# A selective-scan, top-1 expert and feed-forward layer: a new written order of the steps in the steady batches and in the last two and a half

## The reference

```python
delta = softplus(x @ Wd + bd); Bm = x @ WB + bB; Cm = x @ WC + bC; A = -exp(A_log)
# for each token t, state h of 128 x 16:
bar_A = exp(minimum(d_t * A, 2.0)); bar_B = clip(d_t * B_t, -2, 2)
h = clip(bar_A * h + bar_B * x_t, -100, 100)
y = sum(h * C_t, over the 16 states) + x_t * D_param
# for each token y: the most likely of 4 experts
routing = softmax(y @ Wr + br); e = argmax(routing)
moe = (silu(y @ up_w[e] + up_b[e]) @ down_w[e] + down_b[e]) * routing[e]
out = layernorm(y + moe) * ln_w + ln_b
x = layernorm(x + out)
x = layernorm(x + (silu(x @ wg) * (x @ wu)) @ wdn)    # weights are integers / 127
```

## Time and profile before

| | us |
|---|---|
| median of 3 timed runs | 859.77 |
| the three runs | 859.2, 859.77, 875.19 |
| the profiled execution, whole | 854.52 |
| its span, first to last instruction | 852.7 |
| busy: PE, DVE, ACT, POOL | 652.5, 706.2, 517.1, 558.3 |
| first scan to last scan's end | 34.5 to 718.0 |

### The profile page before, as it was taken

One profiled execution on the slowest core, in us unless ns is written; L12 is line 12 of the kernel. 1 busy time (PEld: TensorE's weight loads), 2 busy tenths in 40 slices (PEclk: granted clock), 3 DMA queues, 4 the chain that ended last, 5 costly groups with the idle time before them and its releaser, 6 DMA issues.

```text
span 852.7 us, 14265 instructions
## 1 busy us (share of the span) xinstructions
PE 652.5 (77%) x4267; PEld 529.3 (62%) x4322; DVE 706.2 (83%) x1458; ACT 517.1 (61%) x970; POOL 558.3 (65%) x452
## 2 busy tenths in 40 slices
PE   3366567876789768995889778986988668889686
PEld 1144345864588547874688557964787447778555
DVE  3699999889999999799999999999979999324452
ACT  5274084777577946775777847784678413575534
POOL 1257458658875887578865886588766886525442
PEclk9587696997799959996799869995999859799988
DMA  3333346785467637674578536764667465375410
GB/s 110 123 127 121 127 146 208 244 265 163 146 221 241 204 118 229 201 214 169 171 236 249 177 120 223 237 210 154 209 190 228 140 198 185 107 219 181 132 37 26
DMA packets 82088, 149.32 MB, mean 175 GB/s; under 512 B 9404, under 2 KB 51144, under 8 KB 81992
## 3 DMA queue, kind: packets, MB, share of 16 engines
q1 hardware_dynamic: 69192, 135.13, 49.7%
q0 software_dynamic: 4096, 8.40, 3.1%
q10 hardware_dynamic: 8704, 4.72, 1.9%
HBM read 132.80 MB, written 15.40 MB: 174 GB/s over the span
## 4 chain that ended last, share of the span: by engine, by line
PE 32%; DVE 30%; issue 13%; POOL 12%; ACT 6%; DMA 5%; DVEq 1%; SPq 1%; another core or an unknown queue 0%; POOLq 0%; ACTq 0%
DVE state L1304 8%; DVE state L1318 7%; PE psU L767 6%; POOL prod L1350 5%; PE psT L781 5%; PE psY L637 4%; DVE psB L1299 4%; PE psD L661 3%; POOL rows_in L1371 3%; DMA xT_sb<-in_xT 2%; DMA weights<-in_w_pack 2%; DVE attn L1271 2%; PE psU L808 2%; PE psB L631 2%; PE psU L810 2%
## 5 line engine op out<-in xcount | busy, mean ns | idle before, releaser
L1350 POOL TENSOR_TENSOR prod<-state,c_wide 128x1024 f32<-128x1024 f32 x128 | 302.0, 2367 | 129.7 <-DVE state L1318 109.1
L1299 DVE TENSOR_TENSOR psB<-dx,psB 128x512 f32<-128x512 f32 x256 | 166.7, 684 | 19.3 <-PE psB L631 9.6
L631 PE MATMUL psB<-parts,sel 128*128 128x512 bf16 x202 | 94.0, 470 | 109.7 <-DVE state L1318 65.0
L893 ACT ACTIVATE decay<-delta,a_sb 128x1024 f32<-128x1024 f32 x128 | 141.4, 1141 | 50.1 <-DVE state L1318 48.8
L637 PE MATMUL psY<-ident,prod 128*128 128x128 f32 x1024 | 169.5, 323 | 2.6 <-DVE state L1318 1.5
L1318 DVE TENSOR_TENSOR_SCAN state<-decay,state,psB 128x512 f32<-128x512 f32 x128 | 163.3, 1276 | 8.7
L637 PEld LDWEIGHTS psY<-ident,prod 128*128 128x128 f32 x1024 | 152.0, 170 | 11.6 <-issue 7.9
L1304 DVE TENSOR_TENSOR_SCAN state<-decay,psB 128x512 f32<-128x512 f32 x128 | 155.2, 1213 | 0.1
L934 ACT ACTIVATE hid<-psU,weights 128x128 f32<-128x128 f32 x352 | 100.2, 370 | 50.1 <-PE psU L767 48.4
L631 PEld LDWEIGHTS psB<-parts,sel 128*128 128x128 bf16 x256 | 26.3, 103 | 160.7 <-DVE state L1318 92.7
L767 PE MATMUL psU<-yT_sorted,weights 128*128 128x128 f32 x704 | 95.8, 280 | 10.1 <-DMA weights<-in_w_pack 4.1
(11 more groups left out here) (163 smaller groups left out, 1030.0 us busy)
## 6 DMA issues: line engine op xcount, KB each, us to landing
c_wide<-c_rows SPq DMA_DIRECT2D x128, 512.0 KB, 5.0
weights<-in_w_pack SPq DMA_DIRECT2D x88, 514.0 KB, 4.0
xT_sb<-in_xT SPq DMA_DIRECT2D x8, 512.0 KB, 4.6
y_sorted<-rows_in SPq DMA_DIRECT2D x16, 256.0 KB, 3.3
xt<-in_x SPq DMA_DIRECT2D x8, 512.0 KB, 5.6
...
```

What stands on the lines that cost most here:

```text
L631: pe.matmul(tokens(psB, c, h), sel[:, s, :], parts[:, c.n % 2, h * HALF:h * HALF + c.hw], start=True, stop=True).then_inc(b_ready, 1)
L893: nc.scalar.activation(decay[:, g % NDECAY, w], delta[:, n % 2, w], ACT.Exp, scale=a_sb[:, s:s + 1]).then_inc(decay_ready, 1)
L1299: v.tensor_tensor(tokens(psB, c, h), dx[:, n % 2, h * HALF:h * HALF + c.hw], tokens(psB, c, h), ALU.mult).then_inc(inp_ready, 1)
L1350: g_.tensor_tensor(prod[:, g % NPROD, w], state[:, g % NSTATE, w], c_wide[:, g % NC, w], ALU.mult).then_inc(prod_ready, 1)
```

## The change

Only the ten lists change; no step is added or removed, and each step's instructions and waits stay as they are. Against the list before, a steady batch n (scans of n, expert part of n-1, feed-forward of n-2, preparation of n+1) differs so:

- DVE: b_max goes from behind scan(9) to behind scan(8); centre(1) from ahead of scan_rest(9) to behind scan_rest(10), ahead of bc_low; router_pick, stats(0,2) and aggr(0,2) go ahead of scan_rest(11); dx from behind scan(13) to behind scan_rest(12).
- POOL: prod(2) two gathers earlier; gather(7) ahead of prod(5); x_shift(0) behind prod(12), x_shift(1) behind prod(13).
- ACT: z_copy and softplus later among the decays; decay(11) ahead of norm(0,1), decay(12) behind it, widen ahead of x_low(0); decay(14) from behind silu(3) to ahead of sort_copy(0); x_scaled from behind result(0) to behind sort_copy(2); sort_copy(1) and bc_mid ahead of silu(2); x_high(1) ahead of silu(5).
- SP: c(8) ahead of rows; weights(0) to weights(2) together behind c(4); x later; c rows a place earlier or later.
- PE: b_turn ahead of spread(5,0); ff_up(0,5) ahead of sort_turn(0); sort_turn(1), sort_turn(2), spread(10,1), spread(11,0) one or two places earlier; down(4) ahead of add(10); spread(14,0) from ahead of ff_up(1,1) to behind ff_up(1,4), past b_spread(1) and ff_down(1).

In the last lists (batches 5, 6, 7): combine(0), stats and aggr of batch 5 go from behind scan(14) and scan_rest(15) into scans 10 to 12 of batch 7, combine(1) behind the last scan_rest; SP issues store(0) of batch 6 behind weights(10) and store(1) behind weights(0) of batch 7; PE does ff_down(0) of batch 6 behind ff_up(0,1), ff_down of batch 7 behind ff_up(h,3). The other moves there are of a place or two.

The diff, cut to its core ("..." marks what is left out):

```diff
 PE_ORDER = [
...
-    (-2, "spread", 14, 0), (-4, "ff_up", 1, 1), (-3, "down", 6), (-3, "up", 7), (-1, "b_spread", 1),
...
+    (-2, "spread", 9, 1), (-4, "ff_up", 0, 5), (-3, "sort_turn", 0), (-3, "up", 0), (-2, "spread", 10, 0),
...
+    (-4, "ff_up", 1, 0), (-4, "ff_up", 1, 1), (-3, "down", 6), (-3, "up", 7), (-1, "b_spread", 1),
+    (-4, "ff_up", 1, 2), (-4, "ff_down", 1), (-4, "ff_up", 1, 3), (-4, "ff_up", 1, 4), (-2, "spread", 14, 0),
...
 ACT_ORDER = [
-    (-5, "sort_copy", 2), (-5, "silu", 3), (-4, "decay", 14), (-4, "decay", 15), (-6, "norm", 1, 1),
...
-    (-3, "decay", 12), (-5, "x_low", 0), (-2, "widen"), (-3, "decay", 13), (-5, "gate", 0, 0), (-5, "gate", 0, 1),
-    (-5, "gate", 0, 2), (-4, "sort_copy", 0), (-4, "silu", 0), (-4, "silu", 1), (-4, "result", 0), (-2, "x_scaled"),
-    (-4, "silu", 2), (-2, "bc_mid"), (-4, "result", 1), (-4, "sort_copy", 1), (-4, "result", 2),
...
+    (-6, "gate", 0, 2), (-4, "decay", 14), (-5, "sort_copy", 0), (-5, "silu", 0), (-5, "silu", 1), (-5, "result", 0),
+    (-5, "sort_copy", 1), (-3, "bc_mid"), (-5, "silu", 2), (-5, "result", 1), (-5, "sort_copy", 2), (-3, "x_scaled"),
+    (-5, "result", 2), (-5, "silu", 3), (-4, "decay", 15), (-6, "norm", 1, 1), (-5, "result", 3), (-5, "silu", 4),
...
 DVE_ORDER = [
...
-    (-2, "scan", 9), (-1, "b_max"), (-4, "ff_mul", 0, 2), (-4, "centre", 1), (-2, "scan_rest", 9), (-2, "scan", 10),
-    (-2, "scan_rest", 10), (-1, "bc_low"), (-4, "affine", 1), (-4, "stats", 1, 1), (-4, "aggr", 1, 1),
...
-    (-2, "scan", 12), (-2, "scan_rest", 12), (-2, "scan", 13), (-1, "dx"), (-3, "router_pick"), (-2, "scan_rest", 13),
...
+    (-2, "scan", 8), (-1, "b_max"), (-4, "stats", 1, 0), (-2, "scan_rest", 8), (-4, "aggr", 1, 0),
...
+    (-2, "scan", 10), (-2, "scan_rest", 10), (-4, "centre", 1), (-1, "bc_low"), (-4, "affine", 1),
+    (-4, "stats", 1, 1), (-4, "aggr", 1, 1), (-2, "scan", 11), (-1, "bound", 0), (-3, "router_pick"),
+    (-4, "stats", 0, 2), (-4, "aggr", 0, 2), (-2, "scan_rest", 11), (-2, "scan", 12), (-2, "scan_rest", 12),
+    (-1, "dx"), (-2, "scan", 13), (-2, "scan_rest", 13), (-1, "bound", 1), (-1, "over"), (-4, "ff_mul", 1, 0),
...
 POOL_ORDER = [
...
-    (-6, "rstd", 1, 1), (-4, "prod", 10), (-6, "rstd", 0, 2), (-5, "x_shift", 0), (-4, "prod", 11), (-4, "prod", 12),
...
+    (-5, "prod", 9), (-4, "bound_input"), (-7, "rstd", 1, 1), (-5, "prod", 10), (-7, "rstd", 0, 2), (-5, "prod", 11),
+    (-5, "prod", 12), (-6, "x_shift", 0), (-5, "prod", 13), (-6, "x_shift", 1), (-5, "prod", 14), (-7, "rstd", 1, 2),
...
 SP_ORDER = [
...
-    (-6, "weights", 2), (-6, "rows"), (-5, "c", 8), (-5, "c", 9), (-5, "c", 10), (-6, "weights", 3), (-5, "c", 11),
...
+    (-6, "c", 6), (-6, "c", 7), (-6, "c", 8), (-7, "rows"), (-6, "c", 9), (-7, "weights", 3), (-6, "c", 10),
...
 PE_LAST = [
...
-    (-1, "down", 10), (-2, "ff_down", 0), (-2, "ff_up", 0, 0), (-2, "ff_up", 0, 1), (-2, "ff_up", 0, 2),
...
+    (-1, "down", 10), (-2, "ff_up", 0, 0), (-2, "ff_up", 0, 1), (-2, "ff_down", 0), (-2, "ff_up", 0, 2),
...
 DVE_LAST = [
...
-    (-3, "combine", 0), (-3, "combine", 1), (-1, "scan_rest", 14), (-1, "scan", 15), (-1, "scan_rest", 15),
...
+    (-1, "scan_rest", 9), (-1, "scan", 10), (-3, "combine", 0), (-1, "scan_rest", 10), (-1, "scan", 11),
+    (-3, "stats", 0, 0), (-1, "scan_rest", 11), (-1, "scan", 12), (-3, "aggr", 0, 0), (-1, "scan_rest", 12),
...
+    (-1, "scan_rest", 15), (-2, "router_pick"), (-3, "combine", 1), (-3, "stats", 1, 0), (-3, "centre", 0),
...
 SP_LAST = [
...
-    (-2, "weights", 6), (-2, "weights", 7), (-2, "store", 0), (-2, "weights", 8), (-2, "weights", 9),
...
+    (-2, "weights", 7), (-2, "weights", 8), (-2, "weights", 9), (-2, "weights", 10), (-2, "store", 0), (-1, "rows"),
+    (-2, "x"), (-1, "weights", 0), (-2, "store", 1), (-1, "weights", 1), (-2, "store", 2), (-1, "weights", 2),
...
```

More of the change, by code:

```diff
@@ L70 @@
 PE_ORDER = [
-    (-2, "spread", 11, 0), (-3, "down", 2), (-2, "spread", 11, 1), (-3, "sort_turn", 2), (-3, "up", 3),
-    (-4, "ff_down", 0), (-4, "ff_part", 0, 0), (-1, "b_spread", 0), (-4, "ff_part", 0, 1), (-2, "add", 8),
-    (-4, "ff_part", 0, 2), (-3, "down", 3), (-2, "add", 9), (-2, "spread", 12, 0), (-3, "up", 4),
-    (-2, "spread", 12, 1), (-3, "up", 5), (-2, "add", 10), (-3, "down", 4), (-2, "spread", 13, 0), (-4, "x_turn", 1),
-    (-2, "spread", 13, 1), (-3, "up", 6), (-2, "add", 11), (-4, "x_rest", 1), (-3, "down", 5), (-4, "ff_up", 1, 0),
@@ new lines @@
+    (-2, "spread", 9, 1), (-4, "ff_up", 0, 5), (-3, "sort_turn", 0), (-3, "up", 0), (-2, "spread", 10, 0),
+    (-3, "up", 1), (-2, "spread", 10, 1), (-3, "down", 0), (-3, "sort_turn", 1), (-3, "up", 2), (-3, "down", 1),
+    (-2, "spread", 11, 0), (-3, "sort_turn", 2), (-2, "add", 7), (-3, "down", 2), (-2, "spread", 11, 1),
+    (-4, "ff_down", 0), (-3, "up", 3), (-1, "b_spread", 0), (-4, "ff_part", 0, 0), (-2, "add", 8),
+    (-4, "ff_part", 0, 1), (-4, "ff_part", 0, 2), (-3, "down", 3), (-2, "spread", 12, 0), (-3, "up", 4),
@@ L104 @@
 ]
 DVE_ORDER = [
-    (-4, "stats", 0, 0), (-2, "scan_rest", 4), (-4, "aggr", 0, 0), (-2, "scan", 5), (-4, "centre", 0),
-    (-4, "affine", 0), (-4, "stats", 0, 1), (-2, "scan_rest", 5), (-4, "aggr", 0, 1), (-2, "scan", 6),
-    (-2, "scan_rest", 6), (-2, "scan", 7), (-1, "delta"), (-2, "scan_rest", 7), (-4, "combine", 1), (-2, "scan", 8),
-    (-4, "stats", 1, 0), (-2, "scan_rest", 8), (-4, "aggr", 1, 0), (-4, "ff_mul", 0, 0), (-4, "ff_mul", 0, 1),
-    (-2, "scan", 9), (-1, "b_max"), (-4, "ff_mul", 0, 2), (-4, "centre", 1), (-2, "scan_rest", 9), (-2, "scan", 10),
@@ L116 @@
-    (-2, "scan", 15), (-2, "scan_rest", 15), (-1, "scan", 0), (-1, "scan_rest", 0), (-1, "scan", 1),
-    (-1, "scan_rest", 1), (-1, "scan", 2), (-2, "router_shift"), (-1, "scan_rest", 2), (-2, "slots"), (-1, "scan", 3),
-    (-3, "combine", 0), (-1, "scan_rest", 3), (-1, "scan", 4),
+    (-2, "scan", 4), (-4, "stats", 0, 0), (-2, "scan_rest", 4), (-4, "aggr", 0, 0), (-2, "scan", 5),
+    (-4, "centre", 0), (-4, "affine", 0), (-4, "stats", 0, 1), (-2, "scan_rest", 5), (-4, "aggr", 0, 1),
+    (-2, "scan", 6), (-2, "scan_rest", 6), (-2, "scan", 7), (-1, "delta"), (-2, "scan_rest", 7), (-4, "combine", 1),
@@ new lines @@
+    (-3, "affine", 0), (-3, "stats", 0, 1), (-3, "aggr", 0, 1), (-1, "router_shift"), (-3, "aggr", 1, 0),
+    (-1, "slots"), (-3, "centre", 1), (-3, "affine", 1), (-3, "ff_mul", 0, 0), (-3, "stats", 1, 1),
+    (-3, "aggr", 1, 1), (-3, "ff_mul", 0, 1), (-3, "ff_mul", 0, 2), (-3, "stats", 0, 2), (-3, "aggr", 0, 2),
+    (-3, "ff_mul", 1, 0), (-3, "ff_mul", 1, 1), (-3, "ff_mul", 1, 2), (-2, "combine", 0), (-2, "stats", 0, 0),
+    (-2, "aggr", 0, 0), (-2, "centre", 0), (-2, "affine", 0), (-2, "stats", 0, 1), (-2, "aggr", 0, 1),
```

202 lines of the change are left out of this document (97 added, 105 removed), and 6 rows, old and new, of the table SP_ORDER.

## The result

| | before | after |
|---|---|---|
| median of six runs, us | 861.64 (859.2 to 875.19) | 868.23 (866.6 to 871.69) |
| profiled execution, us | 854.52 | 871.69 |
| its span, us | 852.7 | 869.9 |

The ratio is 1.0092, with a 95% interval of 1.0063 to 1.0121. By the 2% bound this is no change, but the interval lies wholly above 1, and 868.2 is above the forecast's range (838 to 863). The two profiled executions stand 17.2 apart, the medians 6.6: the profiled execution of before is faster than each of its six timed ones, and that of after is the slowest of its six. So the profiles are read for places, and what a place costs is taken from timed ratios. Two of the experiments (e6 and e10) had a disturbed profiled execution; only their times are used.

The account below looks back on a forecast made before the run. DVE was taken as near its limit in the steady periods, PE not far behind, the tail a PE, ACT and weight-DMA chain. Gains of 10.0 + 1.5 = 11.5 from 854.5 gave 843.0, plus 5.3 for the median: 848, range 838 to 863.

Parts of the forecast that it names:

- the stall of 2.1: DVE's affine(1), stretched 2.1 us by GpSimd's bound_input each steady period; forecast gone, with 0.1 us margin, chance 0.40.
- The first rival: Bound_input enters between affine's third and fourth step, so the stall stays: 852.5, 858 as a median; chance 0.33.
- the group's 1.32 is no longer ahead: DVE before bc_low: scan_rest(10) ends at about 425.9, since centre(1)'s 1.32 us now comes behind it.
- the first two batches: Start of the run, ahead of the steady periods: change of 0, within 1 us.
- delta in the steady periods: DVE's delta meets the end of prod(5), now behind gather(7): a cost of 0.2 us a period.
- The 49 table loads: ACT table changes rise from 39 to 49, 1283 ns each; cost nothing if ACT's idle covers them.
- dx's wait: DVE's dx is freed of prod(12): 1.1 us won, but for nothing, since bound(1) waits for PE's b_spread(1).
- The last lists: Tail after the steady periods: -1.5 us, from -4 to +3, by weight DMAs and ff_down(0); last scans nothing.
- a period gains 2.0: Each steady period is 2.0 us shorter, bounds 0 to 3.2; five periods give 10.0.
- the third rival: Slower: bound(0) waits for bound_input after late x_scaled, through uncovered table changes and PE's lower clock; 864.5, median 870; chance 0.14.
- the second: Rival: more goes than one stall (dx's 1.1, PE's lower clock, tail); gain 23, 831.5, 837 as a median; chance 0.13.
- PE's clock behind down(3): PE's fall to 1.2 of 2.4 GHz in two of five periods may go: 0 to 4 us, taken as 0.

Follow-up runs that it names:

- e6: Kernel after with gather(7) back behind prod(5), in five batches: 864.3 us, 0.9833 of before.
- e10: Kernel after with affine(1) ahead of bc_low, x and both x_shifts in their old places, gather(7) back behind prod(5): 859.0 us, no ratio.
- e4: Kernel after with decay(14) ahead of decay(15), 39 table loads again: 868.7 us, 1.0081 of before.
- e9: Kernel after with x_scaled one place later on ACT, behind result(2): 856.7 us, 0.9922 of before.
- e3: Kernel after with the x DMA and both x_shifts in their old places: 864.7 us, 1.0014 of before.
- e14: Kernel before with centre(1) behind scan_rest(10), in five batches: 872.1 us, 1.0112 of before.
- e15: Kernel after with affine(1) ahead of bc_low and centre(1), stats(0,2), aggr(0,2), router_pick in their old places: 883.2 us, 1.0254 of before.
- e11: Repeat of e6, kernel after with gather(7) back behind prod(5): 859.4 us, 0.9967 of before.
- e2: Kernel after with affine(1) ahead of bc_low, in five batches: 856.4 us, 0.9940 of before.
- e5: Kernel before with the change's last lists, steady lists old: 863.0 us, 0.9979 of before.
- e1: Kernel before with affine(1) ahead of bc_low in the five steady batches: 849.5 us, 0.9871 of before.
- e17: Kernel after with affine(1) ahead of bc_low and the x DMA and both x_shifts in their old places: 849.9 us, 0.9854 of before.

## Why the prediction was wrong

**The step that failed** is "If it comes behind the last affine step's start (429.4), the stall of 2.1 is gone ... I take this case". From bc_low's end I had put bound_input at 0.9 and the last step's start at 1.0; they came at 0.65 and 0.83 (bc_low ends 438.78; 439.43 and 439.61). In four of the five steady periods the entry was between the third and the fourth step. The one where x_scaled ended later shows the other side; DVE's and GpSimd's timelines of the period from 476.8:

```profile
534.58 1.14 DVE L1272 SCALAR_TENSOR_TENSOR attn<-moe,rstd,xt 128x128 f32<-128x128 f32 x4
```

```profile
535.78 2.37 POOL L1362 TENSOR_TENSOR bnd<-sp,zb 128x1024 f32<-128x1024 f32 x1 [3.71 <-ACT zb L883]
```

My sum had the entry on the losing side by 0.1, and I still gave the winning side 0.40 against 0.33. The Trainium skill, SBUF — State Buffer, section "Who interferes with whom", was quoted there to the same end, that the pair is held for one whole instruction. The Trainium skill says this there of DVE's 2-port modes, and of an instruction with two SBUF inputs that it contends with GpSimd's reads. The traces of after, e4 and e9 agree for such steps: 2.45 us for a step inside whose group bound_input starts, 0.35 for one ahead of it.

**The first rival's own price was too low.** "The stall stays" was put at 858, and the change came at 868.2, beyond the range. Four terms were missing from it or too small. Their prices overlap (e3 moves the first and perhaps part of the third), so they are not to be added up:

- over behind prod(13): 0.78% or 7 us by e3, which puts back the x DMA and both x_shifts. The prediction said nothing of the x DMA's later place, nor what is queued behind x_shift(0) on GpSimd; the rule to cost every moved step's wait by what stands behind it would have found it.
- centre(1) behind scan_rest(10): "the group's 1.32 is no longer ahead" saw only that DVE's sum stays. PE lives on what scan_rest(10) and the steps before it released until bound(0) frees its bank, and that stretch grew from 9.6 to 11.1 us (434.83 to 445.88). e14 shows the price alone, 1.1% in the old kernel, and e15 what the place buys. What it costs inside the change was not isolated: in the four periods with the stall PE's idle there is 2.5 in the mean instead of 2.2.
- the first two batches: "0, within 1". They took 8.8 more in this profile, and about 5 more in the mean of several. delta met a whole product there in after and e11 and not in e2 and e9, whose order is the same.
- delta in the steady periods: 0.2 charged, 0.45 measured, 1.3 more in five periods.

**Forecast rightly.** The 49 table loads and their price of nothing (e4). dx's wait, won for nothing: dx takes 1.20 now, 3.6 less in the five periods, and DVE's idle before bound(1) grew by 5.3. (It was 1.1 in three of the five periods only.) DVE's idle before b_spread(1), "near 2" (2.06). Centre's meeting with prod(9), 0.2 (1.50 against 1.32). The last lists, -1.5, or 0.2%: e5 measured 0.2%, which can't be told from 0, so that agreement may be luck. The size of a stall: "a period gains 2.0, five periods: 10.0"; e1 gained 8.7 in the steady periods of the profiles, and 1.3%, 11, by the timed ratio.

**The other rivals.** In the steady periods bound(0) never waited for bound_input (once in the second batch, 1.0 at 161.47), so the third rival's mechanism did not occur there, though its side of zero did, and its 870 was nearest to the time. (Its "3 to 4 more on six groups" is 3.2 to 5.3 by the rows it goes by: 0.53 to 0.88 each.) Of the second, a gain of 23, nothing came: with both conflicts out, e17 stands 1.5%, some 13 us, under the kernel before.

PE's clock behind down(3), at "0, I can't tell", came out so: two of five periods at the lower level there, before and after. What the prediction had nothing on is bc at the head of the period, at the lower level in four periods of this execution of after, with DVE waiting 4.4 behind it. It may be chance as much as order.
